# Cross attention: a token tile's maxima turned by four matmuls of 32 stationary columns in place of one of 128

## What is computed

```python
q = (x @ Wq).reshape(B, N, HEADS, hd).transpose(0, 2, 1, 3)        # B = 4, N = 512, 16 heads of 16
k = (context @ Wk).reshape(B, M, HEADS, hd).transpose(0, 2, 1, 3)  # M = 1024
v = (context @ Wv).reshape(B, M, HEADS, hd).transpose(0, 2, 1, 3)
scores = jnp.einsum('bhid,bhjd->bhij', q, k) * scale
scores = jnp.where(context_mask[:, None, None, :], scores, max_neg)
attn = jax.nn.softmax(scores, axis=-1)
out = jnp.einsum('bhij,bhjd->bhid', attn, v)
return out.transpose(0, 2, 1, 3).reshape(B, N, DIM) @ Wo
```

## Time and profile before

| | |
|---|---|
| median of 3 runs | 1227.64 us (1222.44 to 1227.86) |
| profiled execution | 1227.34 us |
| span of its core | 1225.5 us |
| mean granted TensorE clock | 0.979 |
| PE busy | 1140.7 us (93%) |
| PE weight loads | 682.4 us (56%) |
| DVE busy | 950.6 us (78%) |
| ACT busy | 612.4 us (50%) |
| POOL busy | 376.5 us (31%) |
| the 60 transposes of L1477 | 5.9 us busy, 221 ns mean |

### The profile page before, as it was taken

How to read it: one execution, slowest core, us unless ns; L and a number is a source line. 1 busy time by engine, 2 the same in 40 slices (tenths; PEclk the granted TensorE clock), 3 DMA queues, 4 the chain that set the end, 5 groups by cost and what they waited for, 6 DMA issues and landing times. The chain is left out here.

```text
span 1225.5 us, 29594 instructions
## 1 busy us (share of the span) xinstructions
PE 1140.7 (93%) x11646; PEld 682.4 (56%) x11647; DVE 950.6 (78%) x1733; ACT 612.4 (50%) x1166; POOL 376.5 (31%) x361
## 2 busy tenths in 40 slices
PE   7899899999999999889999999999999847999996
PEld 5576666676677777643443344334443333666665
DVE  5889968987888788788788778877889364767757
ACT  4333333343333433237777767777788621444443
POOL 3322255223422222113201220221000444666651
PEclk9899999999999999999999999999999977999999
DMA  7100025000400000025810670173140170221215
GB/s 248 40 1 2 2 56 106 1 2 1 81 1 2 1 2 2 1 59 83 160 24 9 122 139 2 34 131 79 42 172 2 52 199 27 64 64 60 68 56 207
DMA packets 61928, 73.64 MB, mean 60 GB/s; under 512 B 14336, under 2 KB 53376, under 8 KB 61168
## 3 DMA queue, kind: packets, MB, share of 16 engines
q1 hardware_dynamic: 58016, 61.56, 21.0%
q0 software_dynamic: 3792, 10.36, 2.7%
HBM read 52.86 MB, written 18.78 MB: 58 GB/s over the span
## 5 line engine op out<-in xcount | busy, mean ns | idle before, releaser
L1725 DVE TENSOR_REDUCE neg_max<-pS 128x1 f32<-128x1024 f32 x238 | 284.9, 1220 | 51.2 <-PE pS L1508 51.0
L1640 ACT ACTIVATE pt<-pR 128x512 f32<-128x512 f32 x512 | 286.5, 600 | 73.6 <-PE pR L1531 68.5
L1531 PE MATMUL pR<-qs,ks 100*32 100x512 bf16 x2048 | 190.2, 382 | 1.9 <-ACT pt L1640 1.6
L1508 PE MATMUL pS<-ks,qs 100*32 100x512 bf16 x1904 | 145.2, 380 | 3.3 <-DVE neg_max L1725 1.8
L1545 PE MATMUL b_pO<-pt,b_v 128*32 128x512 f32 x1024 | 134.6, 600 | 2.2 <-ACT pt L1640 1.6
L406 PE MATMUL pP<-w_feat,a_xT 128*128 128x512 f32 x244 | 117.2, 604 | 0.7 <-ACT w_feat L682 0.7
L298 POOL TENSOR_TENSOR kf<-kf,fsum 128x2048 f32<-128x2048 f32 (+1 forms) x17 | 58.1, 3420 | 169.5 <-DVE fsum L873 169.5
L1531 PEld LDWEIGHTS pR<-qs,ks 100*32 100x32 bf16 x2048 | 56.1, 96 | 94.6 <-issue 24.4
L298 POOL TENSOR_TENSOR qs<-qs,fsum 128x2048 f32<-128x2048 f32 (+1 forms) x17 | 58.5, 3446 | 144.9 <-DVE fsum L873 144.9
L709 ACT COPY qfT<-pT 128x512 f32<-128x512 f32 x64 | 37.2, 582 | 128.3 <-PE pT L434 128.3
L1387 POOL COPY qs<-max_rows 3x512 bf16<-3x512 bf16 x60 | 36.5, 609 | 209.4 <-ACT max_rows L1633 206.3
(11 more groups left out here) (348 smaller groups left out, 2140.3 us busy)
## 6 DMA issues: line engine op xcount, KB each, us to landing
ks<-k_scr SPq DMA_DIRECT2D x8, 768.0 KB
qs<-q_scr SPq DMA_DIRECT2D x24, 256.0 KB
k_scr<-f SPq DMA_DIRECT2D x18, 256.0 KB, 2.8
ks<-k_scr SPq DMA_DIRECT2D x8, 512.0 KB
ks<-in_L_ffn_w_dram SPq DMA_DIRECT2D x2, 2048.0 KB, 10.6
ks<-in_L_ffn_w_dram SPq DMA_DIRECT2D x4, 1024.0 KB, 8.4
ks<-y_rows SPq DMA_DIRECT2D x16, 256.0 KB, 5.2
cx<-in_ctx_dram SPq DMA_DIRECT2D x3, 768.0 KB, 11.5
```

The source lines that it names most:

```text
L1508: ins = pe.matmul(pS1[q:q + XV, slot, 512 * half:512 * half + 512], qs[0:KR, bass.ds(par, 1), h, P * t + q:P * t + q + XV].rearrange("r a ...
L1531: ins = pe.matmul(ring[bank][q:q + XV, :], ks[0:KR, bass.ds(par, 1), h, P * j + q:P * j + q + XV].rearrange("r a n -> r (a n)"), qs[0:KR, ...
L1640: nc.scalar.activation(pt[:, j % 2, i, :], ring[bank], ACT.Exp).then_inc(exp_done, 1)
L1725: nc.vector.tensor_reduce(neg_max[:, hg % 2, u // G, u % G:u % G + 1], pS1[:, u % 2, :], AX_X, ALU.max, negate=True).then_inc(max_done, 1)
```

## The change

In m_turn each of the four transposes of a 128-column tile becomes four transposes of 32 of its columns, each written to 32 partitions of the same bank. The bank's contents, the waits and the one signal behind the last instruction stay as they were.

```diff
                         for t in range(TB):
-                            ins = pe.transpose(pM[:, 64 * t:64 * t + 64].bitcast(BF16),
-                                               max_parts[:, t, :, :].rearrange("p h v -> p (h v)"),
-                                               ident_h[:, :])
+                            of_tile = max_parts[:, t, :, :].rearrange("p h v -> p (h v)")
+                            for c in range(0, P, XV):
+                                ins = pe.transpose(pM[c:c + XV, 64 * t:64 * t + 64].bitcast(BF16),
+                                                   of_tile[:, c:c + XV], ident_h[:, :])
```

## The result

The changed kernel took 1228.97 us in the median of 20 runs (1224.12 to 1232.89); the kernel before, in 20 runs on the same chip, 1226.67 (1222.44 to 1229.28). The ratio is 1.0022, with an interval of [1.0013, 1.0031]: **slower, by 2.3 us between the medians and 2.7 us by the ratio**, where 0.8 us faster was forecast. The time lies within the range that was given and within 0.5% of no change, but the interval excludes the forecast's sign.

The account below looks back on a forecast made before the run. PE was taken to bound cross attention, streaming without holes; of 3.2 us saved, 0.48 + 0.21 + 0.12 = 0.8 us was to arrive, giving 1226.8 us after allowing for the runs' median; range 1221.8 to 1229.4.

Parts of the forecast that it names:

- What bounds the stage: Cross attention, 565 to 960 us: PE streams with no holes, so its work sets the time unless DVE or ACT is level.
- The seams: PE's losses before and after each turning's transposes, 0.12 and 0.09 us, both expected to go with the change.
- Do the loads keep up: Weight loads of the 32-column transposes on PE: four load side by side, under the 0.06 us a set streams; cost zero.
- rivals 2, 3 and 5: On PE: loads in turn or seams staying, no change, chance 0.15 together; sixteen transposes in sequence, 7.8 us slower, 0.03.
- Place by place: The fifteen turnings in cross attention: how much of each one's 0.21 us reaches the end; 0.8 us in sum.
- the four places with ACT level: Turnings at 650.0, 764.8, 879.5 and 925.8 us: only the transposes' earlier end counts, 0.12 us each, 0.48 in all.
- the one with a step between: Turning at 902.6 us: four f32 transposes precede the next weighted values, whose loads wait for nothing; full 0.21 us gained.
- the nine others: Six turnings with DVE late behind them and three that themselves wait: the saving becomes waiting, 0 gained.
- Rival 1: All turnings in cross attention: the whole saving of 3.2 us arrives, giving 1224.4 us; chance 0.10.
- POOL's copies: POOL's four copies, needed by the next group's scores: no new bound, as PE comes at most 0.2 us earlier.
- What it removes, adds and moves: On PE: 180 matmuls and 180 weight loads more, same waits, both seams gone: 0.21 us per turning, 3.2 in all.
- Rival 4: Clock falls otherwise in the expert stage, 1021 to 1027 us: 2.4 us either way, 1224.4 or 1229.2; chance 0.12.

Follow-up runs that it names:

- the kernel with the filler: The changed kernel plus 64 tiny unread matmuls and their loads at the end of PE's linear attention: 1223.28 us, 0.9973 of the kernel before.
- the two further profiles: The changed kernel measured again, unaltered, in two later comparisons with the kernel before: 1230.56 us, ratio 1.0039, and 1230.37 us, ratio 1.0032.
- the one with the late load: The changed kernel with SP holding back the load of the second batch's q operand: 1241.6 us, 14.4 over the change's profiled execution.

## Why the prediction was right or wrong

- **What bounds the stage**: right but not whole. PE was busy 391.10 of 395.00 us, and I called that "no holes". The 3.90 us missing held the two standstills, 1.73 us of them; asking what the hole at 582.65 was, with no partner to blame, could have led to the cause. The trace that was at hand had it.
- **The seams**: right. 0.12 and 0.09 us forecast, 0.12 and 0.10 measured in the turning at 925.
- **Do the loads keep up**: right. Sets stand 0.056 us apart, rivals 2, 3 and 5 fall. The Trainium skill ("TensorEngine Tiling (Array Packing)", Restrictions) has the rule that column tiling disables Fast Weight Load, which speaks against the change; it cost nothing that a row here shows.
- **Place by place**: right. Lined up work by work with before, the four places with ACT level gave 0.12 us each, the one with a step between 0.22, the last 0.10, the nine others 0 to within 0.02: 0.8 forecast, 0.76 in the kernel with the filler, whose standstills don't fall on these places. Rival 1, all of 3.2 us, falls. One reading was wrong: the wait for DVE at 679.16 was 0.23 us before, not 0.12, which is how long the loads took the earlier trace rows; it grew to 0.48, by about the 0.2 that were forecast.
- **POOL's copies** were no new bound, as said.
- **"What it removes, adds and moves": the step that failed.** 180 matmuls and 180 weight loads more were priced by their execution alone, and on the engine they are indeed free. That they also have to reach PE was never asked. They make a packet more, but that is not the cost. The cost is that from the first turning on, every boundary of 256 lies 24, 48, and in the end 360 instructions earlier in the work. In this part PE works off 507 records in 18.7 us (559.8 to 578.5), 27 a microsecond, so 24 instructions are 0.9 us: the first standstill should grow from 1.38 to 2.3, and it was 2.25, and 2.59 and 2.61 in the two further profiles. At the second, 48 are 1.8 us, less the 0.9 by which PE is late already: 0.35 + 0.9 = 1.25, measured 1.41, 1.14 and 0.95.
- **The rivals**: none of the five was it. The one on the slower side was a price on PE's array, and there was none on the way to PE. So the sum (-0.8) lacked a term of +2.8, with scatter.
- **Rival 4**, the clock: its size was right, its place was not the one named. It lay ahead of the expert stage: from the last weighted values of cross attention to its last matmul (974.93 to 982.85 us before) it took 7.9 us in some profiles and 10.3 in others, whichever kernel (12.0 in the one with the late load). So it explains scatter among runs, 2.4 us. The difference of medians in the first comparison is as large as what the stage itself shows.
- **The range** held 1228.97, but by the clock's term, for a reason that was not the one at work.
- **What would show it wrong** was said to be a change of several us from 565 to 960, and that is what came.

## What to carry to other kernels

Where an engine has less idle time than its program's packets can be late, the number of its instructions is a cost of its own: look for idle time marked "issue" in the middle of a set, and for a data load issued just before it. Such a cost moves with every instruction that is added or taken out anywhere ahead, so a small gain or loss (here 0.2 to 0.4%) may be no property of the edit; it is worth a trial with some filler where the engine is idle anyway, and again after every later edit. And a profile whose bound engine is "99% busy" still has a last per cent: name each of its holes before calling the stage full.

## What the runs showed of the hardware that I had not expected

- PE's program arrives in packets of 16384 bytes, one per about 256 records, over the DMA engines that also carry data. Behind a load of the scores' operands one started 5.6 to 10.0 us after PE had reached the place where it was due, in all of the 31 standstills; with no load about, mostly within some thirty records of it.
- PE runs dry two blocks of 256 records after a boundary at which a packet came in time, and goes on 1.2 to 1.8 us after the late one's end. The Trainium skill ("Runtime: NRT & Kernel Launch", Instruction fetch mechanics) calls the crossing of such a boundary mostly hidden. By that rule the trace agrees where no load runs, and not behind one: up to 2.7 us.
- Two kernels that differ by 128 instructions of filler in an idle place stand at 0.9973 [0.9963, 0.9984] and 1.0032 [1.002, 1.0044] of before: 7 us of 1227.
- Transposes into 32-column tiles run side by side at the full rate: sixteen in 0.41 us, sets of four 0.056 us apart, as four whole ones.
- A standstill of 2.6 us was followed by 3.4 us at the lower clock (0.57 from 589.0 to 592.4) in one profile of three, which added 1.7 us. That the standstill brought it is not shown: the kernel before has such a stretch, 0.72 from 541 to 547 us, with no standstill ahead of it.
